# The attention output's bias: added once to the rows in DRAM instead of on each read

## The reference, cut to what matters

```
h  = layernorm(x)
x1 = x + softmax(clip((h Wq + bq)(ctx Wk + bk)^T * scale)) (ctx Wv + bv) Wo + bo     # 16 heads
g  = layernorm(x1) W1 + b1
q  = g + phase * w_imag * sin(theta + 0.1 g) * 0.1
out = x1 + relu(q) W2 + b2                                                             # 512 -> 2048 -> 512
```

## Time and profile before

| what | value |
|---|---|
| median of 3 runs | 1963.59 us (1960.86 to 1963.77) |
| the profiled execution's own time | 1960.05 us |
| its span, first to last instruction | 1958.0 us |
| PE busy | 1940.6 us |
| DVE, ACT, POOL busy | 1493.0, 1263.5, 549.9 us |
| DMA moved | 468.55 MB, 239 GB/s on average |
| granted TensorE clock, mean | 0.999 |

### The profile page before, as it was taken

How to read it: one execution, slowest core, us unless ns; L and a number is a source line. 1 busy time by engine, 2 the same in 40 slices (tenths; PEclk the granted TensorE clock), 3 DMA queues, 4 the chain that set the end, 5 groups by cost and what they waited for, 6 DMA issues and landing times.

```text
span 1958.0 us, 27871 instructions
## 1 busy us (share of the span) xinstructions
PE 1940.6 (99%) x9162; PEld 1622.7 (83%) x9162; DVE 1493.0 (76%) x2308; ACT 1263.5 (65%) x2132; POOL 549.9 (28%) x391
## 2 busy tenths in 40 slices
PE   9999999999999999999999999999999999999999
PEld 7788888888888788788888888888888888888887
DVE  8988888888876986787578768758757876875763
ACT  6767767667664877577377557647737755764761
POOL 7877777777775321000000000000000000000000
PEclk9999999999999999999999999999999999999999
DMA  7456565566544999899899898998989989898845
GB/s 245 143 163 163 153 166 156 150 176 165 146 116 146 335 347 306 257 297 290 275 309 270 264 311 264 285 278 292 289 278 305 268 267 310 265 283 246 251 151 193
DMA packets 361186, 468.55 MB, mean 239 GB/s; under 512 B 165968, under 2 KB 201808, under 8 KB 361040
## 3 DMA queue, kind: packets, MB, share of 16 engines
q1 hardware_dynamic: 346448, 439.44, 71.0%
q0 software_dynamic: 13728, 27.26, 7.6%
q10 hardware_dynamic: 864, 0.04, 0.0%
HBM read 347.90 MB, written 91.23 MB: 224 GB/s over the span
## 4 chain that ended last, share of the span: by engine, by line
PE 89%; DVE 4%; ACT 2%; DMA 2%; POOL 2%; issue 1%; SPq 0%; POOLq 0%; ACTq 0%; DVEq 0%
PE psum L1999 29%; PE psum L2001 29%; PE psum L2000 29%; PE psum L2092 3%; DMA w_ring<-w1s 1%; DMA x_dram<-res 0%; POOL prob L946 0%; POOL prob L967 0%; DVE stats L1493 0%; DVE top L1629 0%; DVE prob L1620 0%; DVE acc L1846 0%; DVE xt_lo L1729 0%; POOL sums L541 0%; DMA x_sb<-in_x 0%
## 5 line engine op out<-in xcount | busy, mean ns | idle before, releaser
L1999 PE MATMUL psum<-w_ring,act_hi 128*128 128x512 f32 x1024 | 398.7, 389 | 1.6 <-DVE act_lo L1831 1.5
L2000 PE MATMUL psum<-w_ring,act_hi 128*128 128x512 f32 x1024 | 398.4, 389 | 0.0
L2001 PE MATMUL psum<-w_ring,act_lo 128*128 128x512 f32 x1024 | 398.4, 389 | 0.0
L1999 PE MATMUL psum<-xo,w_ring 128*128 128x512 f32 x784 | 305.8, 390 | 2.8 <-ACT p_sb L1365 2.5
L2000 PE MATMUL psum<-xo,w_ring 128*128 128x512 f32 x784 | 305.5, 390 | 0.0
L2001 PE MATMUL psum<-xo,w_ring 128*128 128x512 f32 x784 | 305.5, 390 | 0.0
L1810 DVE SCALAR_TENSOR_TENSOR frac<-frac,turns 128x512 f32<-128x512 f32 x256 | 174.5, 691 | 79.6 <-ACT frac L1358 79.6
L1999 PEld LDWEIGHTS psum<-w_ring,act_hi 128*128 128x128 f32 x1024 | 192.3, 188 | 43.2 <-issue 3.4
L2001 PEld LDWEIGHTS psum<-w_ring,act_lo 128*128 128x128 f32 x1024 | 192.3, 188 | 40.0
L2000 PEld LDWEIGHTS psum<-w_ring,act_hi 128*128 128x128 f32 x1024 | 192.3, 188 | 39.6
L1395 ACT ACTIVATE frac<-frac 128x512 f32<-128x512 f32 x256 | 156.1, 626 | 104.4 <-DVE frac L1810 104.4
(11 more groups left out here) (190 smaller groups left out, 4349.8 us busy)
## 6 DMA issues: line engine op xcount, KB each, us to landing
w_ring<-w2s SPq DMA_DIRECT2D x240, 512.0 KB, 4.3
w_ring<-w1s SPq DMA_DIRECT2D x392, 256.0 KB, 6.1
x_sb<-turn_dram SPq DMA_DIRECT2D x58, 512.0 KB, 6.7
res<-in_x SPq DMA_DIRECT2D x64, 256.0 KB, 3.9
x_dram<-res SPq DMA_DIRECT2D x64, 256.0 KB, 3.1
acc<-x_dram SPq DMA_DIRECT2D x16, 1024.0 KB, 7.6
x_sb<-in_x SPq DMA_DIRECT2D x15, 1024.0 KB, 6.3
x_sb<-x_dram SPq DMA_DIRECT2D x15, 1024.0 KB, 7.9
```

Of the source, the lines that this page charges most:

```text
L1999: pe.matmul(o, a_hi, b_hi, start=first, stop=False, skip_group_check=resumed)
L2000: pe.matmul(o, a_hi, b_lo, start=False, stop=False, skip_group_check=resumed)
L2001: return pe.matmul(o, a_lo, b_hi, start=False, stop=last, skip_group_check=resumed)
```

## The change

`bo` is added to the rows in DRAM. Once the four blocks of a tile are stored, POOL issues one accumulating transfer per tile from `bo_row` (broadcast over four blocks) onto the tile in `x1_dram`, 1 MB each, sixteen in all, and each waits for the landing of the one before it. Tiles 0 to 13 (`GUARDED`) follow in POOL's attention loop at the end of step 4t + 11; tiles 14 and 15 come after the power for the first FFN tile and ahead of `last_done`. Every load of x1 waits for the transfer of its tile. The additions at L904, L910, L1121, L1131 and L1851 go, and the residual in `acc` gets b2 alone.

```diff
+        def biased_tile(i):
+            t, late = divmod(i - LAG_A - 2 * KC - 1, KC)
+            return t if t >= 0 and not late else None
...
 # SP, at n == NB * GUARDED + 1
                     sp.wait_ge(guard_done, 1)
+                    sp.wait_ge(x1_biased, 16 * 2)
...
 # SP, load_rows(T)
                 if T >= GUARDED:
                     sp.wait_ge(last_done, 2)
-                    for blk in range(NB):
-                        sp.wait_ge(x1_stored[blk], 16 * TILES)
+                sp.wait_ge(x1_biased, 16 * (T + 1))
                 sp.dma_start(x_sb[T % 2][:], x1_rows[T]).then_inc(x_in[T % 2], 16)
 # SP, load_acc(T)
+                sp.wait_ge(x1_biased, 16 * (T + 1))
                 sp.dma_start(acc[:, T % 2], x1_rows[T]).then_inc(acc_in[T % 2], 16)
...
 # POOL
-            def add_first_bias(n):
-            def add_row_bias(T, half):
+            def add_bias_rows(t):
+                for blk in range(NB):
+                    pool.wait_ge(x1_stored[blk], 16 * (t + 1))
+                if t:
+                    pool.wait_ge(x1_biased, 16 * t)
+                pool.dma_start(x1_rows[t], bo_row[:].unsqueeze(1).to_broadcast([P, NB, C]), accum_op=ALU.add)\
+                    .then_inc(x1_biased, 16)
...
 # POOL, end of attention step i
+                if biased_tile(i) == 0:
+                    pool.wait_ge(bo_in, 16)
+                if biased_tile(i) is not None:
+                    add_bias_rows(biased_tile(i))
...
 # POOL, after guard_done
-            for n in range(NB):
-                add_first_bias(n)
             rsqrt(TILES)
-            pool.wait_ge(shift_rows_done, TILES + 1)
-            for half in range(2):
-                add_row_bias(1, half)
+            for t in range(GUARDED, TILES):
+                add_bias_rows(t)
...
             pool.memset(ones[:], 1.0).then_inc(last_done, 1)
...
                 if j == 4:
                     pool.wait_ge(b2_in, 16)
-                    pool.tensor_tensor(b2_row[:], b2_row[:], bo_row[:], ALU.add).then_inc(b2_biased, 1)
-                    pool.wait_ge(b2_biased, 1)
...
-                    add_row_bias_by_dma(2 * T + 2)
-                    add_row_bias_by_dma(2 * T + 3)
...
 # DVE, plain steps
-                if j in (6, 7):
-                    add_row_bias(2, j - 6)
...
                 if j in (18, 19):
-                    add_row_bias(3, j - 18)
                     layer_stats(TILES + 3, half_blocks(j - 18))
```

More of the change, by code:

```diff
@@ L312, in xattn_ffn @@
         q_full_done, halves_done = sem("q_full_done"), sem("halves_done")
-        x1_whole = sem("x1_whole")
         xt_psum, xt_hi_done, xt_lo_done = sem("xt_psum"), sem("xt_hi_done"), sem("xt_lo_done")
@@ L335, in xattn_ffn @@
         t_done, xo_hi_done, xo_lo_done = sem("t_done"), sem("xo_hi_done"), sem("xo_lo_done")
-        acc_in, acc_biased, b2_biased = sems("acc_in", 2), sem("acc_biased"), sem("b2_biased")
-        rows_added, out_added = sems("rows_added", 2), sems("out_added", 2)
+        acc_in, acc_biased = sems("acc_in", 2), sem("acc_biased")
+        x1_biased, out_added = sem("x1_biased"), sems("out_added", 2)
         SPLIT0 = 2 * KC
@@ L495, in turned_at @@
             return TURNED_TILES + T - 1
-        def whole_rows(T, half):
-            return NB + 2 * (T - 1) + half + 1
         def plain_events():
@@ L1007, in uniform @@
                 added(pool.tensor_tensor(tile, tile, u_row.unsqueeze(1).to_broadcast([P, tile.shape[1], C]), ALU.add))
+                added(pool.tensor_tensor(tile, tile, bo_row[:].unsqueeze(1).to_broadcast([P, tile.shape[1], C]), ALU.add))
                 for blk in range(tile.shape[1]):
@@ L1091, in _ @@
                 mean_outputs()
-                for blk in range(NB):
-                    pool.wait_ge(x1_stored[blk], 16 * GUARDED)
+                pool.wait_ge(x1_biased, 16 * GUARDED)
                 for t in range(GUARDED):
@@ L1096, in _ @@
             pool.memset(ones[:], 1.0).then_inc(guard_done, 1)
-            for n in range(NB):
-                add_first_bias(n)
             rsqrt(TILES)
-            pool.wait_ge(shift_rows_done, TILES + 1)
-            for half in range(2):
-                add_row_bias(1, half)
+            for t in range(GUARDED, TILES):
+                add_bias_rows(t)
             spare = kt[:].bitcast(F32).rearrange("p g s c -> p (g s) c")
             with pool.If_ne(count, P):
-                for blk in range(NB):
-                    pool.wait_ge(x1_stored[blk], 16 * TILES)
+                pool.wait_ge(x1_biased, 16 * TILES)
                 for m in range((TILES - GUARDED) * NB):
@@ L1128, in _ @@
                     rsqrt(TILES + 3)
[L1129 to L1132, removed]
             def add_last_bias_by_dma(T):
@@ L1140, in _ @@
                 more = T + 1 < FFN_PAIRS
-                if more:
-                    add_row_bias_by_dma(2 * T + 2)
                 add_last_bias_by_dma(2 * T)
                 if more:
-                    add_row_bias_by_dma(2 * T + 3)
                     rsqrt(TILES + 2 * T + 2)
@@ L1485, in layer_stats @@
                     if T == TILES:
-                        dve.wait_ge(x1_whole, n + 1)
-                    elif T > TILES + PLAIN + 1:
-                        dve.wait_ge(rows_added[T % 2], 16 * ((T - TILES) // 2 - 1))
+                        dve.wait_ge(first_in[n], 32)
                     elif T > TILES:
-                        dve.wait_ge(x1_whole, whole_rows(T - TILES, n // 2))
+                        dve.wait_ge(x_in[T % 2], x_loads(T))
                     if T == 0:
@@ L1846, in add_outputs @@
                     dve.tensor_tensor(rows, psum[:, Y2_BANK + n, :], rows, ALU.add).then_inc(y2_done, 1)
[L1848 to L1852, removed]
             def add_last_bias(T, half):
@@ L1856, in add_last_bias @@
                 if T == 0:
-                    dve.wait_ge(b2_biased, 1)
+                    dve.wait_ge(b2_in, 16)
                 rows = acc[:, T % 2, half_rows(half), :]
```

## The result

The changed kernel takes 1970.04 us, the median of five executions; the kernel before takes 1962.96 us, the median of six. The ratio is 1.004 with a 95% interval of 1.0028 to 1.0051: slower by 7.1 us. The forecast was +5.7 us, 1969.3 on the scale of 1963.59, with a range of 1962.0 to 1976.0. The profiled execution after took 1970.04 us as well (span 1967.9).

The account below looks back on a forecast made before the run. PE was taken as the bound, busy 1940.6 of 1958.0 us. Terms -0.3 + 0 - 1.6 + 0 + 0.1 + 5.5 + 2.0 = +5.7 us gave 1969.3 us on the scale of the 1963.59 median, range 1962.0 to 1976.0.

Parts of the forecast that it names:

- The weight wait: Strassen stage: twelve accumulating transfers removed, off the path; PE's one wait on a weight load goes, -0.3 us.
- The change of stage: Four POOL additions before tile 0's statistics removed; PE's next work still needs xt_lo: 0, other end a 1.0 us gain.
- DVE's additions: Plain FFN steps: four DVE additions removed, so both PE waits on act_lo go, -1.6 us; j = 18, 19 give nothing.
- Attention: Transfers of tiles 0 to 13 in POOL's loop, covered by 2.45 us idle read at step 31: 0, far end +14.
- sign that it was wrong: New PE waits between 100 and 590 us, one of the signs named as refuting the forecast; no size given.
- The term for tile 13: Its transfer falls into attention's last step, where POOL mostly waits for ACT's exponential: +0.1 us, bounds 0 to 1.3.
- last_done, +5.5: Tile 14's landing (12.0 us) and tile 15's issue delay last_done; PE stalls at second(0), +5.5 us, ends +1.1 and +10.9.
- Contention by tile 15: Its transfer, 640 to about 653 us, shares full DMA engines with awaited weight chunks and sums: +2.0 us, bounds 0 and +5.9.
- rival (a): Tile 14 lands before the last store, so only tile 15's issue delays last_done: sum +0.3, 1963.9 us; chance 0.20.
- Rival (b): Relief of DVE and DMA shortens PE's 2.5 us wait on p_sb after the plain steps: -4.2, 1959.4 us; chance 0.06.
- Rival (c): Attention transfers delay turned rows or POOL's scaling about 1 us in 14 tiles: +14 on top, 1983 us; chance 0.05.
- Rival (d): Work merely moved, both versions hidden and waits at last_done covered: time unchanged, 1963.6 us; chance 0.07.

Follow-up runs that it names:

- Kernel 6: Changed kernel with attention transfers (tiles 0 to 12) one step earlier, at step 4t + 10, and tiles 13 to 15 after the plain steps' loop; 1955.97 us.
- kernel 8: The kernel before without DVE's four additions of bo (L1851), so rows of tiles 2 and 3 lack bo; 1959.99 us.
- kernel 4: Changed kernel with every attention transfer (tiles 0 to 13) one step later, tile t following step 4t + 12; 1987.99 us.
- kernel 2: Changed kernel with only tile 15's transfer moved after the plain steps' loop; last_done still waits for tile 14 to land; 1965.81 us.
- Kernel 3: Changed kernel, but POOL issues tile 15 without waiting for tile 14's landing; loads of both tiles wait for all sixteen transfers; 1969.44 us.
- Kernel 5: As kernel 2, without the wait for tile 14's landing ahead of last_done; only the stores are awaited; 1964.64 us.
- kernel 1: Changed kernel with the transfers of tiles 14 and 15 moved from ahead of last_done to after the plain steps' loop; 1958.92 us.
- kernels 5 and 7: The second of these is Kernel 6 with guard_done's wait and the loads of tiles 0 and 1 one block later; 1956.38 us.

## Why the prediction held, step by step

The verdict, the sign and the place were right, and the mechanism with them: last_done comes late, and second(0) is where it shows. The sum of +5.7 stands against +7.1 in medians. Its terms:

- **The weight wait, -0.3**: gone, -0.6. **The change of stage, 0**: the four additions before the statistics gave 0.9 us at the transposes, but PE then waited for xt_lo, as the forecast said it must. It did not come out at nothing, but at +0.7: guard_done is set 2.8 us later (614.5 before, 617.35): by then attention itself is 1.9 us behind (0.8 of it chance), and the stretch in which POOL waits for nothing that the profile shows is 5.15 us long and not 4.2 (4.6 to 5.2 in the five kernels with tile 13's transfer at step 63, 4.0 to 4.4 in the four traces without it; why is not shown). With it go the loads of tiles 0 and 1, and all that stands behind them. The forecast called those loads "unchanged"; they were not. Kernel 6 has guard_done at 615.03, and the loss is gone; it moved tile 13 and the step of the others together, so the two are not told apart there.
- **DVE's additions, -1.6**: kernel 8 measured -1.9 in the median, near enough. Besides the two waits that PE's view names there was a hidden gap between them, at 675 us, and the pair at j = 18, 19, to which the forecast gave nothing, gave 0.4 us at 736.
- **Attention, 0 with a far end of +14**: right for tiles 0 to 11. The cover existed, and kernel 4 shows what it was worth: 1.35 us for each tile, by POOL's order alone. Tile 12's transfer (step 59) cost 1.0, with a new wait of PE of 0.7 us on q_lo at 582 us. The forecast had named new waits between 100 and 590 us as a sign that it was wrong; by that sign this term was, once in thirteen tiles. POOL idles only 1.09 and 0.49 us between there and the q_lo that PE awaits next, and that comes 2.1 us later (0.8 of it chance). The forecast looked at step 31 and let it stand for all. The term for tile 13, +0.1, is what the matmuls show at 611 us, but it hides the guard's lateness above.
- **last_done, +5.5**: measured +6.8. The transfer was put at 12.0 us and took 11.90; the issue at 1.3, and it occupied the queue for 1.30. The release was put 5.7 us late and is 9.5 us late, of which about 2.6 is what PE itself had fallen behind by then; the rest is 6.9, and the slack of 0.2 was real. Of the 9.5 us, 3.2 come from tile 14 being issued at 630.27 and not at 627.1: block 59's store lands later when guard_done does.
- **Not in the sum: the clock, +2.7.** After the idle of 6.6 us PE's granted clock is 0.50, the lower of its two levels, 1.2 GHz, for thirteen matmuls: each spacing is longer, by 0.20 us in most. All five executions of the changed kernel in the median show a mean clock of 0.996 or 0.997, against 0.999 to 1.0 of before. The row that would have told it was in the trace of before: behind the wait of 2.5 us on p_sb its clock over 5 us is 0.66.
- **Contention by tile 15, +2.0**: +0.9 at second(1), where ACT had waited 3.2 us for a weight chunk. The whole of tile 15 cost 3.4 by kernel 2, near the 3.3 of the two terms together.

So the size was close by some luck. Of the 9.9 us of the one pair, 0.8 are chance; +2.7 for the clock, +1.7 for the late guard and step 60 and +1.3 at second(0) were missed, and the gains and the contention came out 2.3 us better. The medians lie 2.8 us nearer to each other than that pair, the 0.8 included.

**One reason was wrong though its number was right.** The forecast took the transfers of SP beside tile 14 as small ones that would hardly slow it, and did not ask what it does to them. It blamed the wait for tile 14's landing, and its rival (a) let the last store land when it had landed before, at about 634.7 us. Kernel 3 took that wait out and gained nothing. Kernel 5 took out every wait for the transfer and still lost 6.0 us against kernel 1. What holds the engines is the last store, which lands in 6.5 to 6.9 us when the transfer is in flight. In the trace of before the same thing can be read: the store at 618.19, issued behind the 1 MB load of tile 1, took 8.9 us (L685, stores issued from 616.5 to 618.5 us):

```profile
DMA to landing us min/median/max: 8.9/8.9/8.9
```

Rival (a), that the transfer is quick, did not happen: sixteen took 9.2 to 12.2 us. The Trainium skill's page DMA: Bandwidth & Descriptors, section Anatomy of one DMA, would give 4.4 us by its formula, an estimate; the trace disagrees for accumulation onto DRAM as it had for that into SBUF. Rival (b) has its point of decision in the wait on p_sb, and that stayed at 2.5 in the changed kernel; in kernel 6 it shrank. Rival (c) did not happen; kernel 4 shows its two mechanisms, POOL's order with a price of 1.35 us a tile, the late loads without one. Rival (d), that the slack covers all, fell with the first line of PE's waits.

**What stays open.** Whether the store lands late since its bytes share the DMA engines with the transfer, or since its completion is held back behind the transfer's writes, no run here separates. That the two land within 0.2 us of each other in the changed kernel, and within 0.03 us in kernel 5 (642.54 and 642.57), speaks for the second; in kernel 3 they are 0.5 us apart (641.47 and 641.98). Against a plain holding back until the transfer is done speaks block 62's store, issued 1.9 us behind the transfer in the changed kernel: it landed 2.6 us ahead of it, 3.3 in kernel 3, 2.3 in kernel 5, having taken 7.1 to 7.4 us. The Trainium skill's page DMA: Bandwidth & Descriptors, section Queues, rings and completion order, describes the second: a completion is an ordered write that lands only after every earlier write of its DMA engine, across queues. The runs agree with this without proving it; block 62's store does not contradict it, if fewer of the transfer's writes were ahead of it, which no view here shows. Nor is it settled why the clock fell after waits of 2.1 us (kernels 5 and 7) and 2.5 us (before), and not after 1.9 us (the changed kernel), 2.4 us (kernel 5, at second(0)), 3.2 us (kernel 1) or the same 2.5 us on p_sb in kernel 2.

## What to carry to other kernels

A transfer that nobody waits for can still make somebody wait: before placing a large one, list the small transfers whose landing releases an engine in the next ten microseconds, and look in the trace for what such a one took beside an earlier large one. Check the cover at each place where a periodic step puts its instruction, the last rounds above all: here the same edit is free in step 4t + 10 or 4t + 11, costs 1.35 us a tile in 4t + 12, and costs again in attention's last rounds (tiles 12 and 13). When a stall of PE is forecast, add the matmuls behind it at the lower clock as a term that may or may not come, and read their number from a stall of the trace at hand.

## What the runs showed of the hardware that was not expected

- An accumulating transfer of 1 MB onto DRAM takes 8.9 to 9.7 us where little runs beside it (thirteen in kernel 6), 9.2 to 12.2 in the changed kernel, and up to 16.7 late in the plain steps (kernel 6, issued at 781 us).
- Stores of 128 to 256 KB issued 1.3 to 5.6 us behind its start take 5.3 to 8.6 us where they take 2 to 3; those issued near its end are hardly late (kernel 6: thirteen stores issued 7.2 us behind it, 2.3 to 4.3 us). The stores that carry the rows to be turned (`turn_dram<-kt`, 128 KB, issued both during a flight and outside one), 100 to 545 us: before, then the changed kernel.

```profile
turn_dram<-kt SPq DMA_DIRECT2D x102, 128.0 KB, 2.3
```

```profile
turn_dram<-kt SPq DMA_DIRECT2D x99, 128.0 KB, 3.8
```

- Attention did not feel it at these places: PE was busy 489.30 of 490 us with a DMA share of 0.72. A share is no measure of what a transfer in flight does to the next small one.
- Idle time of PE is charged twice when the clock falls behind it: 6.6 us of waiting brought 2.7 us more.
